# Turning attention probabilities by a trip over DRAM and VectorE instead of TensorE, with scores two tiles ahead

## The chip, the cores and the metric

One core of a Trainium2 chip runs the whole kernel. The metric is the device time of one launch in microseconds. Before the change the median of three runs was 490.21 us (490.07 to 491.41).

## The reference

The input x is 4 batches of 1024 tokens with 512 features, all fp32. Cut to what matters:

```python
mod = (silu(c) @ wmod).reshape(4, 6, 1, 512)        # sa, ca, ga, sb, cb, gb per batch
ga, gb = sign(ga) * max(|ga|, 0.25), sign(gb) * max(|gb|, 0.25)
h = layernorm(x) * (1 + ca) + sa
qf, kf = h @ Wq.T, h @ Wk.T                         # 64 columns each, the same for all 16 heads
attn = softmax(qf @ kf.T)                           # 1024 x 1024 per batch
x = x + ga * ((attn @ (h @ Wv.T)) @ Wo.T)
h = layernorm(x) * (1 + cb) + sb
x = x + gb * (h @ sum_r(factors[r]) / sqrt(8) + bias)
```

All heads share one probability matrix, so Wv and Wo are multiplied once into one 512x512 matrix, and the eight factors are summed once.

## The kernel before

The 4096 tokens are 32 tiles of 128, eight per batch, handled in 16 pairs. fp32 values go through TensorE as two roundings: a high part (`_hi`) and the rest (`_lo`, `rest()` at line 838), and `three()` multiplies hi x lo, lo x hi and hi x hi (lines 373 to 375).

A prologue makes the modulation vectors, the weights and the values and keys of the first batch. Then come 32 steps, one per tile t. Every engine runs its own hand-written order of the same step, and semaphores join them; most steps run in loops (`Fori`). In step t TensorE does, in order:

- `transpose_probs(t)`: eight 128x128 transpositions of the probabilities into two PSUM banks ps_t (line 379);
- in odd steps the query/key projection of a pair of the next batch, and in steps 0 to 23 the value projection of tile t+8;
- the scores of tile t+1 into ps_s (two banks, lines 447 and 448);
- the feed-forward of tile t-3 into ps_y;
- `attend(t)`: 24 matmuls into ps_o, which start when VectorE has made the first half of pt_lo.

ScalarE rounds ps_t to pt_hi (605), modulates x1 of tile t-2 (634), rounds the values, normalizes x1 of tile t-1 (693), modulates x of tile t+9 (634), takes the exponentials of tile t+1 (674, into the only buffer `probs`), and normalizes x of tile t+10 (642). VectorE gates the attention of tile t-1 (918), adds x (926), takes statistics (931, 935), turns x1 and x (961, 957), subtracts for pt_lo and the values' rest (838), takes the row maximum of tile t+1 (890), finishes the feed-forward (951), and splits h and h2 into a cast for the high part (855, 901) and a subtraction for the rest (838). GpSimd makes inverse deviations (1173 to 1177), and multiplies and adds the feed-forward's result (1189, 1192).

x and x1 are already turned by a trip. SP sends the normalized tile in 32-column blocks to DRAM (`blocks_out`, line 301) and fetches it with the blocks in another order (`blocks_in`, line 306); VectorE transposes all 32x32 blocks in one instruction; and ScalarE's modulation reads them in order and writes every fourth element. SP issues these in one queue with the loads of x (245) and stores of the result (252). In a step its order is: fetch x, send x1, store, fetch x1, send x, load.

The gates ga and gb of all four batches are broadcast over the partitions by SP (`spread_gate`, lines 266 and 268) into `gates`, 1 MB each.

Of the kernel before, what the change touches and what calls it, by code (L numbers as in the profile page):

```python
# [20 lines left out]
GATE_MADE = [12, 18]  # L21


def adaln_block(nc, x, wqk_t, wv, wo_t, factors, bias, c_t, wmod, out):
# [29 lines left out]
    assert (P, D, R, C, TB, B) == (128, 512, 64, 4, 8, 4) and KEYS == 2 * D  # L54
# [5 lines left out]
    x1_blocks = nc.dram_tensor("x1_blocks", [2, Q, P, P], F32, kind="Internal").ap()  # L60

    with ExitStack() as ctx:
# [24 lines left out]
        negmax = sb("negmax", [P, 2])  # L87
        rowsum = sb("rowsum", [P, 2])
        rden = sb("rden", [P, 2])
        bias_bc = sb("bias_bc", [P, D])  # L90
# [11 lines left out]
        gates = sb("gates", [P, 2, B, D])  # L102
        mod_rows = gates[0:B].rearrange("b a c d -> b (a c) d")
# [12 lines left out]
        with ExitStack() as setup:  # L116
            sb("under_parts", [P, TB, D], F32, setup)
            w_parts = [sb("w_part_0", [P, C, D], F32R, setup), sb("w_part_1", [P, C, D], F32R, setup)]
            sb("under_more", [P, TB, D], F32, setup)
            w_parts += [sb("w_part_2", [P, C, D], F32R, setup), sb("w_part_3", [P, C, D], F32R, setup)]  # L120
            sb("under_last", [P, TB, D], F32, setup)
            w_parts += [sb("w_part_4", [P, C, D], F32R, setup)]
            f_sum = sb("f_sum", [P, C, D], F32, setup)
        wmod_sb = [wmod_0, wmod_1, wmod_2]
# [17 lines left out]
        f_lo = sb("f_lo", [P, C, D], F32R)  # L142
        probs = sb("probs", [P, KEYS])
        qs_hi = sb("qs_hi", [P, 2 * P], F32R)
        qs_lo = sb("qs_lo", [P, 2 * P], F32R)
        h2_f = sb("h2_f", [P, C, P])
# [58 lines left out]
        qs_hi_done, qs_lo_done = sem("qs_hi_done"), sem("qs_lo_done")  # L205
        s_acc, max_done, exp_done = sem("s_acc"), sem("max_done"), sem("exp_done")
# [28 lines left out]

        block = ctx.enter_context(nc.Block())
# [3 lines left out]
        def _(sp):  # L240
# [21 lines left out]
            def spread_gate(i, vector):  # L262
# [3 lines left out]
                sp.dma_start(gate_rows[i], mod_rows[:, row_of[vector], :]).then_inc(gate_stored[i], 16)  # L266
                sp.wait_ge(gate_stored[i], 16)
                sp.dma_start(gates[:, i].rearrange("p b d -> p (b d)"), gate_rows[i].rearrange(
                    "b d -> (b d)").partition_broadcast(P)).then_inc(gate_loaded[i], 16)
# [25 lines left out]
            spread_gate(0, GA)  # L295
# [29 lines left out]
            def step(g, u, next_x=True, next_norm=True, store=True, load=False):  # L325
                t = 2 * g + u
                if next_x:
                    fetch_x(t + TB + 1, 1 - u)
                send_x1(t - 1, 1 - u)
                if u and store:  # L330
                    store_pair(g - 2)
                fetch_x1(t - 1, 1 - u)
                if next_norm:
                    send_x(t + TB + 2, u)
                if u and load:
                    wait_alone(sp, sp_passed, y_stored, 16 * (g - 1))
                    load_x(g - 2 + 2 * PB)

            step(0, 1, next_x=False, next_norm=False, store=False)
            step(1, 0, next_x=False, store=False)  # L340
            spread_gate(1, GB)
            step(1, 1, store=False)
            for u in range(2):
                step(2, u, load=True)
            with sp.Fori(3, PAIRS - 2 * PB + 2) as g:
                for u in range(2):
                    step(g, u, load=True)
            with sp.Fori(PAIRS - 2 * PB + 2, PAIRS - PB - 1) as g:
                for u in range(2):
                    step(g, u)  # L350
            step(PAIRS - PB - 1, 0, next_norm=False)
            step(PAIRS - PB - 1, 1, next_x=False, next_norm=False)
            with sp.Fori(PAIRS - PB, PAIRS - 1) as g:
                for u in range(2):
                    step(g, u, next_x=False, next_norm=False)
            step(PAIRS - 1, 0, next_x=False, next_norm=False)
            last = PAIRS - 1
            store_pair(last - 2)
# [10 lines left out]
        def _(pe):  # L369
# [36 lines left out]
            def modulation_columns(n, vectors):  # L406
                for i, v in enumerate(vectors):
                    for k in range(C):
                        at = (i * C + k) * B
                        last = nc.tensor.transpose(mod_t_banks[n][:, at:at + B], mod_rows[:, row_of[v], P * k:P * (k + 1)],  # L410
# [87 lines left out]
            def step(g, u, prep=True, following=True, older=True, late_x=None, ready=None):  # L498


                t = 2 * g + u
                transpose_probs(t)
                if prep and u:
                    pe.wait_ge(h_lo_done, t + TB + 1)
                    project_qk(g + PB)
                if late_x is not None:
                    late_x()
                if prep:
                    project_values(t + TB, u)
                if following:  # L510
                    scores(t + 1, 1 - u, g + u)
                if older:
                    feed_forward(t - 3)
                if ready is not None:
                    ready()
                attend(t, g)

# [56 lines left out]
            step(0, 0, older=False, late_x=transpose_first_late)  # L574
            step(0, 1, older=False, late_x=transpose_second_late, ready=lambda: pe.wait_ge(h_f_done, TB + 3))
            step(1, 0, older=False, late_x=transpose_third_late)
            pe.wait_ge(h_f_done, TB + 4)
            step(1, 1)
            with pe.Fori(2, PAIRS - PB) as g:
                for u in range(2):  # L580
                    step(g, u)
            with pe.Fori(PAIRS - PB, PAIRS - 1) as g:
                for u in range(2):
                    step(g, u, prep=False)
            step(PAIRS - 1, 0, prep=False)

            step(PAIRS - 1, 1, prep=False, following=False)
# [15 lines left out]
        def _(act):  # L603
# [68 lines left out]
            def exponentials(t, u):  # L672
                act.wait_ge(max_done, t + 1)
                nc.scalar.activation(probs[:], ps_s[:], ACT.Exp, bias=negmax[:, u:u + 1],  # L674
                                     accum_out=rowsum[:, u:u + 1]).then_inc(exp_done, 1)

            def probs_part(t, half):
                act.wait_ge(pt_ps, 2 * t + half + 1)
                rounded(pt_hi[:, HALF * half:HALF * (half + 1), :], ps_t[half][:]).then_inc(pt_hi_done, 1)
# [25 lines left out]
            def modulate_x1(t, b):  # L705
                if not isinstance(t, int) or t > 0:
                    wait_alone(act, act_passed, h2_lo_done, t)
                wait_alone(act, act_passed, x1b_turned, t + 1)
                modulate_turned(h2_f, x1b, b, 2).then_inc(h2_f_done, 1)

            def factor_parts():
                for half in range(2):
# [4 lines left out]
            def step(g, u, prep=True, next_x=True, next_norm=True, last_pair=False, after_x=True):  # L717
                t = 2 * g + u
                first = isinstance(g, int) and g == 0
                by_pe = isinstance(t, int) and t + TB + 1 in late_x_banks  # L720
                probs_part(t, 0)
                if prep and u:
                    qk(g + PB)
                probs_part(t, 1)
                if by_pe:
                    modulate_x(t + TB + 1, batch_of(g + u + PB), late_x_banks[t + TB + 1])
                if not first:
                    modulate_x1(t - 2, batch_of(g - 1))
# [589 lines left out]
```

## Time and profile before

| | |
|---|---|
| median of 3 runs | 490.21 us |
| profiled execution | 491.66 us, span 489.5 us |
| mean granted TensorE clock | 0.994 |
| TensorE, VectorE, ScalarE, GpSimd busy | 473.9, 370.0, 282.5, 196.3 us |
| DMA | 62.63 MB, mean 128 GB/s |

Busy time is the union of an engine's instructions; the span runs from the first to the last instruction. The profiled execution is one run, 1.45 us above the median; 2.2 us of it lie around the span. Instructions of one engine overlap by about 0.1 us when they follow each other directly, so a duration is a little more than the distance from start to start.

### The profile page before, as it was taken

The page shows a single profiled execution, that of the slowest core. Times are in us where ns is not written, and L with a number is a line of the kernel's source. Part 1 is how long each engine was busy: PE and PEld are TensorE (multiplying, and loading weights), DVE is VectorE, ACT ScalarE, POOL GpSimd, SP SyncE. Part 2 cuts the span into 40 slices and gives each one's busy share as a digit, 9 for nine tenths or more (in the row PEclk, how much of TensorE's full clock was granted, in tenths as well). Part 3 has the DMA queues.
Part 4 walks back from the last instruction along what each step waited for, and adds up shares of the span by engine and source line. Part 5 has one row for each costly group of instructions (what it writes and reads, how often), then busy time and mean ns, then how long its engine had stood idle before and what let it go on. Part 6 is the DMA issues. An engine that isn't in the chain of part 4 may idle for free.

```text
span 489.5 us, 9481 instructions
## 1 busy us (share of the span) xinstructions
PE 473.9 (97%) x2306; PEld 385.7 (79%) x2306; DVE 370.0 (76%) x688; ACT 282.5 (58%) x579; POOL 196.3 (40%) x286
## 2 busy tenths in 40 slices
PE   8999889999999999999999999999999999999985
PEld 3777658887888888888888888888888888888864
DVE  2896875888886877786878868687877587978775
ACT  2877655577574747466665747474765453554431
POOL 0475763414433424243434334242432533344344
PEclk9999998999999999999999999999999999999999
DMA  8968889754244252525243342535341212132212
GB/s 301 364 255 210 153 157 227 152 140 153 66 129 124 80 160 86 171 72 165 84 130 99 112 130 81 156 86 171 85 129 44 86 44 86 43 97 95 61 49 86
DMA packets 50818, 62.63 MB, mean 128 GB/s; under 512 B 2920, under 2 KB 29288, under 8 KB 50544
## 3 DMA queue, kind: packets, MB, share of 16 engines
q1 hardware_dynamic: 46848, 54.82, 35.1%
q0 software_dynamic: 3808, 7.34, 8.9%
q10 hardware_dynamic: 144, 0.26, 0.1%
q8 instruction: 7, 0.11, 0.1%
q14 instruction: 11, 0.09, 0.1%
HBM read 40.90 MB, written 21.51 MB: 128 GB/s over the span
## 4 chain that ended last, share of the span: by engine, by line
PE 77%; DVE 7%; issue 6%; ACT 3%; DMA 3%; POOL 2%; SPq 0%; ACTq 0%; DVEq 0%; POOLq 0%
PE ps_o L373 11%; PE ps_o L375 11%; PE ps_o L374 11%; PE ps_t L379 6%; PE ps_y L373 5%; PE ps_y L375 5%; PE ps_y L374 5%; PE ps_v L373 5%; PE ps_v L374 4%; PE ps_v L375 4%; PE ps_s L447 3%; PE ps_s L448 3%; PE ps_qk L373 1%; PE ps_qk L375 1%; PE ps_qk L374 1%
## 5 line engine op out<-in xcount | busy, mean ns | idle before, releaser
L373 PE MATMUL ps_o<-v_lo,pt_hi 128*128 (+1 forms) x256 | 100.6, 393 | 1.8 <-DVE pt_lo L838 1.8
L1173 POOL TENSOR_SCALAR ve<-mv 128x1 f32<-128x1 f32 x64 | 14.9, 233 | 216.1 <-DVE mv L935 188.3
L375 PE MATMUL ps_o<-v_hi,pt_hi 128*128 (+1 forms) x256 | 99.8, 390 | 0.0
L374 PE MATMUL ps_o<-v_hi,pt_lo 128*128 (+1 forms) x256 | 99.7, 389 | 0.0
L605 ACT ACTIVATE pt_hi<-ps_t 128x512 fp32r<-128x512 f32 x64 | 36.1, 597 | 75.1 <-PE ps_t L379 74.8
L634 ACT ACTIVATE h_f<-x1b,mod_t 128x128 f32<-128x128 f32 x120 | 53.2, 595 | 44.8 <-DVE x1b L961 44.8
L918 DVE SCALAR_TENSOR_TENSOR attn<-ps_o,rden,gates 128x512 f32<-128x512 f32 x32 | 24.0, 751 | 58.8 <-PE ps_o L375 57.4
L373 PEld LDWEIGHTS ps_o<-v_lo,pt_hi 128*128 128x128 f32 x256 | 48.1, 188 | 14.2 <-issue 3.6
L375 PEld LDWEIGHTS ps_o<-v_hi,pt_hi 128*128 128x128 f32 x256 | 48.0, 188 | 10.1
L374 PEld LDWEIGHTS ps_o<-v_hi,pt_lo 128*128 128x128 f32 x256 | 48.1, 188 | 9.7
L838 DVE TENSOR_TENSOR h_lo<-h_f,h_hi 128x512 fp32r<-128x512 f32 (+1 forms) x67 | 51.5, 782 | 1.2
L373 PE MATMUL ps_y<-f_lo,h_hi 128*128 128x512 f32 (+1 forms) x124 | 48.4, 390 | 0.3 <-DVE h_lo L838 0.3
L375 PE MATMUL ps_y<-f_hi,h_hi 128*128 128x512 f32 (+1 forms) x124 | 47.9, 386 | 0.0
L374 PE MATMUL ps_y<-f_hi,h_lo 128*128 128x512 f32 (+1 forms) x124 | 47.9, 386 | 0.0
L1189 POOL TENSOR_TENSOR ffn<-ffn,gates 128x512 f32<-128x512 f32 x30 | 40.5, 1350 | 16.9 <-DVE ffn L951 15.3
L373 PE MATMUL ps_v<-wvo_lo,h_hi 128*128 128x512 f32 x112 | 45.5, 406 | 0.0
L374 PE MATMUL ps_v<-wvo_hi,h_lo 128*128 128x512 f32 x112 | 44.3, 396 | 0.0
L375 PE MATMUL ps_v<-wvo_hi,h_hi 128*128 128x512 f32 x112 | 44.1, 394 | 0.0
L1192 POOL TENSOR_TENSOR x_ring<-ffn,x_ring 128x512 f32 (+1 forms) x30 | 39.8, 1325 | 10.2 <-POOL ffn L1189 10.2
L674 ACT ACTIVATE probs<-ps_s,negmax 128x1024 f32<-128x1024 f32 x32 | 35.6, 1114 | 12.8 <-DVE negmax L890 12.7
L1175 POOL TENSOR_TENSOR rstd<-ve,minus_half 128x1 f32<-128x1 f32 x64 | 39.9, 623 | 5.3
L838 DVE TENSOR_TENSOR pt_lo<-ps_t,pt_hi 128x512 fp32r<-128x512 f32 x64 | 41.7, 665 | 0.1
(170 smaller groups left out, 1004.4 us busy)
## 6 DMA issues: line engine op xcount, KB each, us to landing
x_blocks<-xn SPq DMA_DIRECT2D x50, 256.0 KB, 2.3
x_ring<-in_x SPq DMA_DIRECT2D x16, 512.0 KB, 3.8
x1b<-x_blocks SPq DMA_DIRECT2D x30, 256.0 KB, 2.7
result<-x_ring SPq DMA_DIRECT2D x15, 512.0 KB, 3.0
f_sum<-in_factors POOLq DMA_DIRECT2D x14, 512.0 KB, 7.3
wmod<-in_wmod SPq DMA_DIRECT2D x12, 512.0 KB, 6.9
xb<-x_blocks SPq DMA_DIRECT2D x20, 256.0 KB, 2.7
gates<-gate_rows SPq DMA_DIRECT2D x2, 1024.0 KB, 6.2
```

What stands on the lines that cost most here:

```text
L373: nc.tensor.matmul(acc, a_hi, b_lo, start=first, stop=False)
L374: nc.tensor.matmul(acc, a_lo, b_hi, start=False, stop=False)
L375: return nc.tensor.matmul(acc, a_hi, b_hi, start=False, stop=last)
L379: last = nc.tensor.transpose(acc[:, P * i:P * (i + 1)], source[:, P * (base + i):P * (base + i + 1)], ident[:])
L605: return nc.scalar.activation(to, source, ACT.Identity)
L634: last = nc.scalar.activation(to[:, k, :].rearrange("p (c b) -> p b c", b=Q), turned[:, k], ACT.Identity, scale=mod_t[:, b, v + 1, k:k + 1 ...
L674: nc.scalar.activation(probs[:], ps_s[:], ACT.Exp, bias=negmax[:, u:u + 1], accum_out=rowsum[:, u:u + 1]).then_inc(exp_done, 1)
L838: return nc.vector.tensor_tensor(to, whole, full(hi), ALU.subtract)
L918: nc.vector.scalar_tensor_tensor(out=attn[:], in0=ps_o[:], scalar=rden[:, u:u + 1], in1=gates[:, 0, b, :], op0=ALU.mult, op1=ALU.mult).the ...
L1175: nc.gpsimd.tensor_tensor(rstd[:, one], ve[:, one], minus_half[:], ALU.pow).then_inc(rstd_done, 1)
L1189: nc.gpsimd.tensor_tensor(ffn[:, 0:D], ffn[:, 0:D], gates[:, 1, b, :], ALU.mult).then_inc(gated_done, 1)
L1192: nc.gpsimd.tensor_tensor(tile, ffn[:, 0:D], tile, ALU.add).then_inc(y_done, 1)
```

## The change

For 24 of the 32 tiles (all but 0 to 4, 8, 16 and 24) the probabilities are no longer turned by TensorE. ScalarE writes the exponentials in 32-column blocks, SP sends them to `p_blocks` in DRAM and fetches them in the other order into `pb` (two slots), VectorE transposes 128x1024 in one instruction at the end of the step before, ScalarE rounds from pb to pt_hi and VectorE subtracts for pt_lo, both with every fourth element.

- Scores: those of tile t+2 are made in step t, after the feed-forward. The first two tiles of a batch are exceptions: the first is scored in the last step of the batch before, ahead of its attention, the second in the same step behind its attention. Its maximum and exponentials open the next step on VectorE and ScalarE.
- The casts of h and h2 to their high parts move from VectorE to ScalarE.
- SP's order in a step: fetch x, fetch probabilities, send x1, store, send probabilities, send x, fetch x1, load.
- The gates are held for two batches at a time: 256 KB are broadcast per gate and batch, the first ones where 1 MB was, the later ones in steps 5, 13 and 21.
- GpSimd multiplies the result ahead of the statistics of x1 and adds it behind them.
- The query parts of a pair are made in odd steps instead of even ones. All steps are unrolled.

```diff
+def turned_by_pe(t):
+    return t <= LAST_EARLY or t % PER_BATCH == 0          # LAST_EARLY = 4, PER_BATCH = 8
+def scored_in(t):
+    if t < LAST_EARLY:
+        u = t + 1
+    elif t % PER_BATCH == PER_BATCH - 2:
+        return None
+    else:
+        u = t + (1 if t % PER_BATCH == PER_BATCH - 1 else 2)
+    return u if u < TILES else None
+def scored_last_in(t):
+    opens = t == LAST_EARLY - 1 or t % PER_BATCH == PER_BATCH - 1
+    return t + 2 if t >= 0 and opens and t + 2 < TILES else None
...
+        def turned_probs(t):
+            return pb[:, trips_of(t) & 1, :].rearrange("p (b k c) -> p k b c", b=Q, c=BLK)
...
+            def spread_gate(i, b):
+                sp.wait_ge(gate_stored[i], 16)
+                if b:
+                    sp.wait_ge(gate_loaded[i], 16 * b)
+                if b > 1:
+                    sp.wait_ge((attn_done, gated_done)[i], TB * (b - 1))
+                sp.dma_start(gates[:, i, b & 1, :], gate_rows[i, b].partition_broadcast(P)).then_inc(gate_loaded[i], 16)
...
+            def send_p(t):
+                n = trips_of(t)
+                sp.wait_ge(exp_done, t + 1)
+                if n > 1:
+                    sp.wait_ge(pb_loaded, 16 * (n - 1))
+                sp.dma_start(p_blocks[n & 1].rearrange("a p x -> p a x"),
+                             probs[:].rearrange("p (a x) -> p a x", a=Q)).then_inc(p_out, 16)
+            def fetch_p(t):
+                n = trips_of(t)
+                sp.wait_ge(p_out, 16 * (n + 1))
+                sp.wait_ge(pt_lo_done, 2 * (t - 1))
+                sp.dma_start(pb[:, n & 1, :],
+                             p_blocks[n & 1].rearrange("a (c b) x -> (a c) (b x)", b=Q)).then_inc(pb_loaded, 16)
...
             # TensorE, a step
+                if turned_by_pe(t):
+                    transpose_probs(t)
...
+                if t >= 3:
                     feed_forward(t - 3)
+                if scored_in(t) is not None:
+                    scores_of(scored_in(t))
                 attend(t, g)
+                if scored_last_in(t) is not None:
+                    scores_of(scored_last_in(t))
...
             # ScalarE
+                to, source = in_quarters(pt_hi)[:, here], turned_probs(t)[:, here]     # a trip tile
...
+            def h_upper(q, u):
+                act.wait_ge(h_f_done, q + 1)
+                rounded(h_hi[:, :, here], h_f[:]).then_inc(h_hi_done, 1)
...
             # VectorE
+                    last = rest(in_quarters(pt_lo)[:, here], turned_probs(t)[:, here], in_quarters(pt_hi)[:, here])
...
+            def turn_p(t):
+                n = trips_of(t)
+                dve.wait_ge(pb_loaded, 16 * (n + 1))
+                nc.vector.transpose(pb[:, n & 1, :], pb[:, n & 1, :]).then_inc(pb_turned, 1)
```

VectorE's new order in a step: maximum of a tile scored last, gate, query/key rest, add, statistics, turn x1, first pt_lo, values, statistics of x, turn x, second pt_lo, maximum, rests of h and h2, feed-forward's end, query parts, turn of pb.

## Rows read from the trace of the kernel before

**Rows 1.** The page, part 1: busy time, share, instructions of each engine.
```profile
PE 473.9 (97%) x2306; PEld 385.7 (79%) x2306; DVE 370.0 (76%) x688; ACT 282.5 (58%) x579; POOL 196.3 (40%) x286
```
**Rows 2.** Stretches: PE, PEld, DVE, ACT, POOL busy, clock, DMA share, GB/s.
```profile
136.32:190.12 53.80, 53.80 (x267) 45.15 (x265) 41.28 (x80) 33.09 (x68) 20.57 (x32) 1.00 0.39 117
392.10:463.20 71.10, 71.10 (x340) 58.20 (x339) 57.74 (x91) 34.58 (x69) 27.05 (x35) 1.00 0.24 71
```
**Rows 3.** Chain that ended last, in order of time: start, us, what.
```profile
190.12 0.87 PE ps_t L379 x8
204.25 0.87 PE ps_t L379 x8
216.93 0.87 PE ps_t L379 x8
```
**Rows 4.** Timeline of TensorE around the transpositions, mid-kernel and tail: start, duration.
```profile
203.85 0.39 PE L375 MATMUL ps_o<-v_hi,pt_hi 128*128 x1
...
204.88 0.48 PE L373 MATMUL ps_v<-wvo_lo,h_hi 128*128 128x512 f32 x1
...
412.23 1.03 PE L379 MATMUL ps_t<-ident,probs 128*128 128x128 f32 x8
...
416.75 0.48 PE L373 MATMUL ps_o<-v_lo,pt_hi 128*128 x1
```
**Rows 5.** Groups of VectorE in 136.32 to 190.12: busy, mean ns, idle before.
```profile
L918 DVE SCALAR_TENSOR_TENSOR attn<-ps_o,rden,gates 128x512 f32<-128x512 f32 x4 | 3.0, 752 | 8.7 <-PE ps_o L375 8.7
...
L926 DVE TENSOR_TENSOR x_ring<-attn,x_ring 128x512 f32 x4 | 2.8, 693 | 1.0 <-DVE attn L918 1.0
```
**Rows 6.** Groups of the whole span, by form.
```profile
L890 DVE TENSOR_REDUCE negmax<-ps_s 128x1 f32<-128x1024 f32 x32 | 38.8, 1214 | 0.0
...
L961 DVE STREAM_TRANSPOSE x1b<-x1b 128x512 f32<-128x512 f32 x30 | 20.9, 696 | 0.3 <-DMA x1b<-x_blocks 0.3
...
L855 DVE CAST h_hi<-h_f 128x512 fp32r<-128x512 f32 x32 | 15.2, 474 | 3.5 <-ACT h_f L610 3.4
...
L605 ACT ACTIVATE w_part<-wmod 128x512 fp32r<-128x512 f32 x12 | 6.6, 629 | 0.0
...
L838 DVE TENSOR_TENSOR v_lo<-wv_raw,v_hi 128x512 fp32r<-128x512 f32 x4 | 2.7, 680 | 6.7 <-ACT v_hi L605 6.7
```
**Rows 7.** Instructions on the tile ps_t: ns min/median/max, first and last start.
```profile
L838 DVE TENSOR_TENSOR pt_lo<-ps_t,pt_hi x64: 650/668/693, 74.9 to 467.2; 128x512 fp32r<-128x512 f32 x64
```
**Rows 8.** Timeline of ScalarE: four modulations, plain and strided.
```profile
99.19 1.51 ACT L610 ACTIVATE h_f<-ps_y,mod_t 128x128 f32<-128x128 f32 x4
...
154.46 1.77 ACT L634 ACTIVATE h_f<-x1b,mod_t 128x128 f32<-128x128 f32 x4 [2.45 <-DVE x1b L961]
```
**Rows 9.** DMA issues of the page: count, KB each, median us to landing.
```profile
x_blocks<-xn SPq DMA_DIRECT2D x50, 256.0 KB, 2.3
x_ring<-in_x SPq DMA_DIRECT2D x16, 512.0 KB, 3.8
x1b<-x_blocks SPq DMA_DIRECT2D x30, 256.0 KB, 2.7
```
**Rows 10.** Timeline of the tail, VectorE and GpSimd.
```profile
398.80 1.29 POOL L1189 TENSOR_TENSOR ffn<-ffn,gates 128x512 f32<-128x512 f32 x1 [1.55 <-DVE ffn L951]
...
398.98 1.66 DVE L838 TENSOR_TENSOR h_lo<-h_f,h_hi 128x512 fp32r<-128x512 f32 x1
...
412.75 0.75 DVE L918 SCALAR_TENSOR_TENSOR attn<-ps_o,rden,gates 128x512 f32<-128x512 f32 x1 [2.71 <-PE ps_o L375]
...
415.93 1.25 DVE L838 TENSOR_TENSOR pt_lo<-ps_t,pt_hi 128x512 fp32r<-128x512 f32 x2
```
**Rows 11.** Timeline around step 3: SP, VectorE and TensorE.
```profile
111.14 0.34 SPq L268 DMA_DIRECT2D gates<-gate_rows  x1
...
116.52 0.71 DVE L957 STREAM_TRANSPOSE xb<-xb 128x512 f32<-128x512 f32 x1 [1.87 <-DMA xb<-x_blocks]
...
117.95 0.47 PE L373 MATMUL ps_o<-v_lo,pt_hi 128*128 128x512 f32 x1 [1.03 <-DVE pt_lo L838]
```

More of the change, by code:

```diff
@@ L21, with pe_turns_of, trips_of, queries_in @@
 GATE_MADE = [12, 18]
+LAST_EARLY = 4
+TILES, PER_BATCH = 32, 8
+def turned_by_pe(t):
+    return t <= LAST_EARLY or t % PER_BATCH == 0
+def pe_turns_of(t):
+    return sum(turned_by_pe(u) for u in range(t))
+def trips_of(t):
+    return t - pe_turns_of(t)
+def scored_in(t):
[9 more added lines that the diff above has]
+    return t + 2 if t >= 0 and opens and t + 2 < TILES else None
+def queries_in(t):
+    pair = (t + 3) // 2 if t % 2 and t >= LAST_EARLY - 1 else t // 2 + 1 if t % 2 == 0 and t < LAST_EARLY - 1 else None
+    return pair if pair is not None and 2 * pair < TILES else None
 def adaln_block(nc, x, wqk_t, wv, wo_t, factors, bias, c_t, wmod, out):
@@ L337, in step @@
+                if u and 2 <= g < PAIRS - 2 * PB + 2:
+                    sp.wait_ge(y_stored, 16 * (g - 1))
                     load_x(g - 2 + 2 * PB)
[L339 to L356, printed above, removed]
+            for t in range(T):
+                step(t)
+                if t == 1:
+                    store_gate(1, GB)
+                if t == 2:
+                    spread_gate(1, 0)
+                if t < T - TB and t % TB == TB - 3:
+                    for i in range(2):
+                        spread_gate(i, t // TB + 1)
@@ L573, in _ @@
             pe.wait_ge(h_f_done, TB + 1)
-            step(0, 0, older=False, late_x=transpose_first_late)
-            step(0, 1, older=False, late_x=transpose_second_late, ready=lambda: pe.wait_ge(h_f_done, TB + 3))
-            step(1, 0, older=False, late_x=transpose_third_late)
+            step(0, transpose_first_late)
+            step(1, transpose_second_late, lambda: pe.wait_ge(h_f_done, TB + 3))
+            step(2, transpose_third_late)
             pe.wait_ge(h_f_done, TB + 4)
[L578 to L587, printed above, removed]
+            for t in range(3, T):
+                step(t)
             pe.wait_ge(x2n_done, T - 1)
@@ L771, in prep_pair @@
                     if u and first_scores:
-                        exponentials(0, 0)
+                        exponentials(0)
                     values(q, prologue_v[u])
@@ L968, in step @@
+            def step(t):
+                g, u = t // 2, t % 2
+                q = t + TB + 1
+                if scored_last_in(t - 1) is not None:
+                    row_max(scored_last_in(t - 1))
+                if t:
+                    gate_attention(t - 1, 1 - u, batch_of((t - 1) // 2))
+                if t < T - TB and u:
+                    qk_rest(g + PB)
+                if t:
                     add_x(t - 1)
                     x1_sums(t - 1, 1 - u)
-                if not first:
+                if t < T - TB and u:
+                    k_rest(g + PB)
+                if t >= 2:
```

356 lines of the change are left out of this document (183 added, 173 removed).

## The prediction

> **What bounds the kernel now.** I read the page first, then stretches, the chain of waits, and the timelines of one step. The page gives TensorE 473.9 us of 489.5, VectorE 370.0, ScalarE 282.5 [rows 1]. An average hides the stages, so next the stretches: over four tiles in mid-kernel (53.80 us) TensorE is busy for all 53.80, VectorE for 41.28, ScalarE for 33.09, DMA for 0.39 of its time; with no projections left (71.10 us) TensorE is still busy throughout [rows 2]. The chain is TensorE's own work, step after step: 14.13 us for a step with a query/key projection, 12.68 for one without [rows 3]; in the tail 71.10/7, about 10.15. What leaves TensorE there is time saved, as long as another engine doesn't take its place.
>
> **Transpositions removed.** Eight of them stand between the attention of one tile and the next work. The last attention matmul starts at 203.85; with the usual 0.23 from start to start the next would follow at 204.08, but the projection starts at 204.88 [rows 4]. That is 0.80; the chain gives the eight 0.87, with what the first matmul behind them loses [rows 3]. I take 0.87. Eight times the duration of one (over 0.27) would say 2.2 and is wrong: matmuls overlap. 24 tiles make 20.9 us as the ceiling. They fall in two stages: tiles 5 to 7, 9 to 15 and 17 to 23 (17) beside projections, tiles 25 to 31 (7) in the tail.
>
> **VectorE, in the first 17.** In the four-tile stretch it waits 8.7 us for the attention's last matmul [rows 5]; so it needs (53.80 - 8.7)/4 = 11.27 us per tile, and has 2.18 free. TensorE's period falls from 13.45 to 12.58, which leaves 1.31. The edits:
> - Two casts per tile go to ScalarE. One takes 474 ns alone [rows 6], less in line; -0.75 for two.
> - A 32x32 transposition of 1024 columns comes. 512 columns take 696 ns; a reduction of 1024 takes 1214 [rows 6]. Bounds 1.13 to 1.39 (twice 696); I take 1.2, the reduction's.
> - The two roundoff subtractions read SBUF instead of PSUM and read and write every fourth element. No strided VectorE row exists. Nearest: an SBUF source without stride, 680 ns beside 668 from PSUM [rows 6, 7]. ScalarE's four strided modulations take 1.77, four plain ones 1.51 [rows 8]: 0.26 over 512 columns, part of it the end of the last. Bounds 0 and a doubled element time, 0.52 (what 512 more columns cost, 1214 - 696 [rows 6]); I take 0.2, two of them 0.4.
> - A new exposure: with two SBUF inputs VectorE can stand behind GpSimd. At 398.98 such a subtraction took 1.66 instead of 0.68; GpSimd's multiplication ran from 398.80 to 400.09, and the rest came after that [rows 10]. None of the 64 subtractions from PSUM went over 693 ns [rows 7]. GpSimd has two 1.3 us operations and small ones per tile. Bounds 0 and 2 x 0.97 = 1.94 per tile; I take one half-hit, 0.5, as GpSimd's addition (after the statistics of x1) falls near the second subtraction.
>
> The Trainium skill, "SBUF — State Buffer", section "SBUF: two separate sides", states it as a rule: a VectorE operation with two SBUF inputs and a GpSimd operation that reads SBUF exclude each other for a whole instruction. The trace agrees (1.66 against 0.68), and by the rule this change is exposed twice per tile: that is the rival that ends slower. The same page's section on the DMA port swizzle puts fp32 strides up to four elements down as free; by it the 0.4 above would be 0. ScalarE's rows (0.26 over 512 columns) speak against quite free.
>
> Sum 11.27 - 0.75 + 1.2 + 0.4 + 0.5 = 12.62 beside TensorE's 12.58. The two meet. Two engines so close that hand each other work lose a little to waiting; I put 0.2 on it, an estimate from the 0.25 that VectorE waits for its own result before an addition, 1.0 over four [rows 5]. So 12.8 instead of 13.45: 0.65 x 17 = 11.1 us.
>
> **ScalarE** in the same stage: 8.27 busy per tile, plus two casts (629 ns from SBUF, 0.53 in line, and 0.2 for its own result: 1.5 together), plus 0.2 to 0.4 on two roundings: about 10.2 to 10.5 of 12.58 [rows 2, 6]. Hidden; if that cover goes, only its place in the cycle below counts.
>
> **The trip.** Scores stand two tiles ahead, so the exponentials of tile t+2 end near the end of step t. 512 KB take 3.8 us [rows 9], out and in 7.6 and some 0.7 of issue and waits, against a step of 12.6; the transposition is the last thing VectorE does in step t+1. Hidden by about 3 us. The new waits and what stands behind them: VectorE's turn of pb waits for the fetch, and behind it the gate and with it the next attention's buffer; SP's sending waits for the exponentials, and behind it stand the sending of x and the fetch of x1; the exponentials wait for the sending before, long landed. If the cover of 3 us goes, each us more is one on VectorE. A megabyte more per tile beside 1.6 now (117 GB/s [rows 2]) lifts the DMA share from 0.39 to some 0.65: no bound.
>
> **SP's order.** Fetching x1 now stands behind the sending of the probabilities and of x. That closes a cycle: fetch 2.7, VectorE's turn 0.7, ScalarE sees it 0.47, modulates x1 1.57, normalizes x1 0.7, modulates x 1.57, casts 0.7 and 0.5, exponentials 1.1, normalizes x 0.75, issues 0.95 in the code's order [rows 6, 8, 9]: 11.7, plus what the 512 KB ahead in the queues adds: 0 to 1.5 (3.8 - 2.3). With 0.5, 12.2, it stays under 12.6. ScalarE waited 2.45 for VectorE's turn before its modulation [rows 8]: the path has slack of that size and no more.
>
> **Batch ends (steps 6 to 8, 14 to 16, 22 to 24).** Scores of a batch's second tile run after the attention of the last tile before. Step 6 loses them (0.91), step 8 gains them: zero. In step 8 VectorE and ScalarE each begin with one more operation (1.2, 1.1), but 6 us of projection and feed-forward lie ahead of the attention; zero.
>
> **The tail.** There VectorE's chain from the attention's end to the first pt_lo decides. The step's transpositions start at 412.23; VectorE's attn starts at 412.75, its first pt_lo at 415.93 and ends near 416.58, 4.35 us after the slot; TensorE starts the attention at 416.75, 4.52 after it [rows 4, 10]. Without transpositions it would be ready at 3.65 and waits for the 4.35. Of 0.87 only some 0.15 is left, with the stride 0.1: six steps, 0.6. Step 31 has no scores, so even now less than 4.35 lies ahead of its attention: nothing. Step 24 gets the second scores (0.91) and VectorE's maximum ahead of gate, add and statistics: attention at about 1.4 + 1.2 + 3.8 = 6.4 instead of 4.52, a loss of 1.9, of which step 22 gave 0.9. Tail and its opening: 0.6 + 0.9 - 1.9 = -0.4.
>
> **The start.** At 111.14 SP issued the 1 MB broadcast of the gates, behind a store that it had waited for, and only then fetched x: the turn of x waited 1.87 us and TensorE 1.03 [rows 11]. The store now stands a step earlier, and 256 KB are broadcast: 1.0 gained. Later broadcasts of 256 KB stand in steps 5, 13, 21: hidden. The unrolled loops I price at 0: no row shows a wait for code, and none excludes one.
>
> **Sum.** 11.1 - 0.4 + 1.0 = 11.7 us. The profiled execution took 491.66 (span 489.5 and 2.2 around it), 1.45 above the median of 490.21; against the median, 478.5.
>
> **Rivals.**
> - Everything hidden: period 12.58, no hits by GpSimd. 14.8 - 0.4 + 1.0 = 15.4: 474.8. For it: VectorE's numbers meet it within 0.1. Against: my sum has VectorE level with TensorE.
> - SP's cycle decides: the full 1.5 us of queueing makes 13.2 per tile. 0.25 x 17 - 0.4 + 1.0 = 4.9: 485. For it: x1's fetch is now the last of SP's step. Against: 256 KB landed in 2.3 to 2.7 in the median, with 512 KB transfers in the same queues [rows 9].
> - Slower: GpSimd's lock hits both subtractions of each tile, 0.97 each. VectorE needs 11.27 + 0.45 + 0.4 + 1.94 = 14.06, against 13.45 before: 0.61 x 17 = 10.4 lost; start and tail give 0.6 back: 500. It decides as soon as a subtraction costs 0.87 more than before ((2.18 - 0.45)/2). For it: 1.66 in rows 10. Against: every one has to be hit, and GpSimd is idle for 33 of 53.80 us (20.57 busy) [rows 2].
> - The change doesn't do what it says (TensorE spared, but each removed slot filled by an equal wait): 490.
>
> **Chances.** Forecast 0.42, everything hidden 0.18, SP's cycle 0.18, no net change 0.07, slower 0.15. The measurement tells 0.3% (1.5 us) from nothing. Faster: 0.42 + 0.18 + 0.17 = 0.77; same 0.08; slower 0.15. The forecast's own range is 474 to 482. Leaving 0.15 above and 0.05 below: 472 to 489.
>
> **What would show it.** Right: a mid-kernel step pair of some 25.6 us instead of 26.81; VectorE busy over 11 us per tile, hardly waiting for the attention's last matmul; tail steps of about 10; the stall at 117.95 gone. Subtractions on pb near 0.85 us with a few at 1.2 to 1.7. Wrong: pt_lo over 1.5 on average (the lock), turns of x1 waiting for DMA in each step (SP's cycle), turns of pb waiting for DMA (the trip isn't hidden), or TensorE idle at the batch ends.

## The result, and the profile after

The changed kernel is slower: 503.5 us (median of 4 runs, 499.85 to 503.82) against 490.14 (median of 4 runs, 489.68 to 491.41) on the same chip, a ratio of 1.025 (95% interval 1.020 to 1.030). Forecast were 478.5 us and a range of 472 to 489. The profiled execution has a span of 502.0 us; before it was 489.5, so 12.5 us are to be explained.

Part 1 of the page after, for [rows 1], and the head of its chain of waits:

```profile
PE 461.0 (92%) x2114; PEld 366.3 (73%) x2114; DVE 400.0 (80%) x659; ACT 339.9 (68%) x632; POOL 216.1 (43%) x286
...
DVE 30%; PE 23%; DMA 17%; issue 13%; ACT 9%; POOL 6%; SPq 1%; ACTq 0%; DVEq 0%; POOLq 0%
```

TensorE is busy 12.9 us less than before, and the span is 12.5 us longer: 25 us of idle time on TensorE are new. No single engine took its place. The chain before was TensorE at 77%; now it goes round over VectorE, DMA, ScalarE and GpSimd.

Which stage? I count a step from one start of `attn` on VectorE to the next. Stretches of the kernel after, cut at the `attn` of tiles 4, 23 and 31; the columns are those of [rows 2]:

```profile
0.00:137.17 137.17, 128.19 (x626) 97.36 (x627) 101.62 (x186) 92.04 (x187) 63.21 (x92) 1.00 0.74 192
137.17:396.70 259.53, 247.77 (x1130) 201.94 (x1129) 220.08 (x355) 194.99 (x355) 106.94 (x147) 0.99 0.57 183
396.70:484.84 88.14, 74.90 (x310) 59.21 (x309) 66.68 (x97) 49.05 (x82) 38.00 (x40) 0.96 0.47 149
484.84:502.00 17.16, 10.13 (x55) 7.81 (x53) 11.65 (x22) 3.83 (x9) 7.94 (x9) 0.92 0.17 63
```

The same cuts before lie at 136.63, 392.45 and 473.16. Inside the 19 steps from tile 4 to tile 23 the steps fall in two kinds, so I part them too: the eight around a batch's end (6, 7, 8, 14, 15, 16, 22, 23) and the 11 others. All numbers are differences of those `attn` starts in the profiled execution:

```
                      start    11 steps (each)    8 steps   tail (8)   end
before               136.63    149.42 (13.58)     106.40     80.71    16.34
after                137.17    148.53 (13.50)     111.00     88.14    17.16
change                +0.5      -0.9               +4.6      +7.4     +0.8
forecast              -1.0      -7.15              -3.9      +0.4      -
```

(The forecast's 0.65 for each of 17 steps: 11 of the first kind, 6 of the second, where steps 8 and 16 keep their transpositions. A negative number is time saved.) So the ordinary step hardly got shorter, by 0.08 us instead of 0.65; counted between the first attention matmuls on TensorE it is 0.27 (13.33 instead of 13.60). The pairs of steps 9+10, 11+12, 17+18 and 19+20 took 26.28, 27.05, 27.28 and 26.84 us, against 26.81 before and a forecast of some 25.6. The batch ends, priced at zero beside the 0.65, and the tail lost 12.0 us.

**The ordinary step** is a closed cycle. One turn of it in the chain of waits of the kernel after (start, us, what), from one fetch of x1 to the next:

```profile
207.24 2.94 DMA x1b<-x_blocks
210.21 0.04 DVE x1b L1067
210.24 0.60 issue
210.84 0.14 DVE mv L1040
210.98 0.57 DVE pt_lo L932
211.56 0.30 issue
211.86 0.68 DVE v_lo L932
212.54 0.60 DVE stats L935
...
213.68 1.70 DVE pt_lo L932
215.38 1.13 DVE negmax L991
...
216.80 1.07 POOL ve L1275
...
217.94 0.58 POOL rstd L1277
...
218.73 0.27 POOL nmr L1279
219.01 0.83 ACT xn L715
...
219.92 0.36 SPq L362
...
220.47 3.04 DMA x1b<-x_blocks
```

From 207.24 to 220.47 are 13.23 us; the turns beside it in the chain took 13.19, 13.05 and 13.81, and the table's eleven steps 13.50 on average. SP issues the fetch of x1 behind the sending of x, which waits for ScalarE's `xn`, for GpSimd's three small operations, for VectorE's `mv` of x (L939); and that stands behind both subtractions (`pt_lo`) and the row maximum, which stand behind the turn of the x1 fetched before. The x1 to be fetched had been in DRAM since about 216.5: SP issued its own sending at 214.09 (x_blocks<-xn lands in 2.4).

**The subtractions.** Instructions on the tile pt_lo after, to be read beside [rows 7]:

```profile
L932 DVE TENSOR_TENSOR pt_lo<-pb,pt_hi x48: 1035/1064/1710, 141.6 to 478.8; 128x512 fp32r<-128x512 f32 x48
L932 DVE TENSOR_TENSOR pt_lo<-ps_t,pt_hi x16: 652/656/691, 74.5 to 400.2; 128x512 fp32r<-128x512 f32 x16
```

The stride costs 0.41 each (1064 against 656; with plain columns, experiment 1, those from pb take 656 too). It lies on pt_lo and pt_hi; pb itself is read in runs of 32. 13 of the 48 stand at 1.5 to 1.71, one in each of 13 mid-kernel steps, always the second, behind GpSimd's addition. From the timeline of the kernel after:

```profile
200.21 1.29 POOL L1297 TENSOR_TENSOR x_ring<-ffn,x_ring 128x512 f32<-128x512 f32 x1
...
200.75 1.69 DVE L932 TENSOR_TENSOR pt_lo<-pb,pt_hi 128x512 fp32r<-128x512 f32 x1
```

**The batch end.** SP's queue in step 6 of the kernel after, and what its chain of waits shows there:

```profile
150.35 0.36 SPq L362 DMA_DIRECT2D x_blocks<-xn  x1
150.89 0.42 SPq L367 DMA_DIRECT2D x1b<-x_blocks  x1
151.44 0.37 SPq L299 DMA_DIRECT2D x_ring<-in_x  x1
151.91 0.91 SPq L329 DMA_DIRECT2D gates<-gate_rows  x2
153.01 0.32 SPq L367 DMA_DIRECT2D xb<-x_blocks  x1
```

```profile
153.01 6.25 DMA xb<-x_blocks
...
159.29 0.04 DVE xb L1063
159.32 0.60 issue
159.93 1.05 DVE pt_lo L932
...
161.02 0.52 PE ps_o L448
```

The two gate broadcasts are issued right ahead of the fetch of x. That fetch of 256 KB, 3.0 us in the median, takes 6.25, and behind the turn of x in VectorE's program stands the second subtraction, for which TensorE idles 2.40 us. The idleness costs once more, as the stretches around it show (the seventh number is the granted clock):

```profile
158.60:161.00 2.40, 0.02 (x1) 0.00 (x0) 1.71 (x3) 0.96 (x3) 0.00 (x0) 1.00 0.81 291
161.00:164.90 3.90, 3.88 (x10) 3.10 (x11) 2.45 (x5) 2.67 (x6) 1.38 (x4) 0.56 0.06 16
164.90:168.00 3.10, 3.10 (x21) 2.79 (x20) 1.47 (x4) 0.89 (x3) 0.97 (x1) 1.00 0.54 154
```

After 2.4 us without work TensorE ran 3.4 of the next 3.9 us at the lower of its two levels (1.2 GHz; matmuls 0.43 apart instead of 0.23): some 1.7 us more.

**The tail.** GpSimd's groups from 396.70 to 484.84 (mean ns, idle before):

```profile
L1277 POOL TENSOR_TENSOR rstd<-ve,minus_half 128x1 f32<-128x1 f32 x8 | 8.7, 1090 | 0.7
L1275 POOL TENSOR_SCALAR ve<-mv 128x1 f32<-128x1 f32 x8 | 6.9, 865 | 39.0 <-DVE mv L1040 39.0
```

The same two took 567 and 222 ns in the kernel before. They work on one column; it is the lock in reverse. In each step both subtractions stand right behind `mv`, and the two short operations come in their time. That is 1.17 us more per step between the statistics of x1 and what follows from x1. In four of the eight steps the chain that ended last runs over them (from 409.42, 421.38, 431.49 and 454.64); in the others it runs over the subtractions and the attention.

### The profile page after: what moved, and what is told of

It reads as the page before. It is cut to its first block, busy times and chain, and to the rows that moved or that the text cites. A ratio compares the mean times of both kernels' runs of the same rounds, so it can differ in the third digit from the quotient of the medians.

```text
span 502.0 us, 7290 instructions
## 1 busy us (share of the span) xinstructions
PE 461.0 (92%) x2114; PEld 366.3 (73%) x2114; DVE 400.0 (80%) x659; ACT 339.9 (68%) x632; POOL 216.1 (43%) x286
## 4 chain that ended last, share of the span: by engine, by line
DVE 30%; PE 23%; DMA 17%; issue 13%; ACT 9%; POOL 6%; SPq 1%; ACTq 0%; DVEq 0%; POOLq 0%
DMA x1b<-x_blocks 8%; DVE pt_lo L932 7%; DMA xb<-x_blocks 6%; PE ps_o L448 4%; PE ps_o L450 4%; PE ps_o L449 4%; DVE negmax L991 3%; DMA x_blocks<-xn 3%; DVE h_lo L932 2%; POOL rstd L1277 2%; ACT xn L715 2%; POOL ve L1275 2%; DVE stats L935 2%; DVE x_ring L1031 2%; ACT probs L755 2%
## 5 line engine op out<-in xcount | busy, mean ns | idle before, releaser
L1275 POOL TENSOR_SCALAR ve<-mv 128x1 f32<-128x1 f32 x64 | 37.1, 579 | 213.3 <-DVE mv L1040 140.5
L448 PE MATMUL ps_o<-v_lo,pt_hi 128*128 128x512 f32 x256 | 104.0, 406 | 25.5 <-DVE pt_lo L932 25.4
L450 PE MATMUL ps_o<-v_hi,pt_hi 128*128 128x512 f32 x256 | 101.9, 398 | 0.0
L449 PE MATMUL ps_o<-v_hi,pt_lo 128*128 128x512 f32 x256 | 101.7, 397 | 0.0
L678 ACT ACTIVATE pt_hi<-pb 128x512 fp32r<-128x512 f32 x48 | 49.1, 1128 | 18.1 <-PE ps_o L450 13.1
L932 DVE TENSOR_TENSOR h_lo<-h_f,h_hi 128x512 fp32r<-128x512 f32 (+1 forms) x67 | 44.3, 688 | 20.3 <-ACT h_hi L678 19.8
L932 DVE TENSOR_TENSOR pt_lo<-pb,pt_hi 128x512 fp32r<-128x512 f32 x48 | 58.3, 1228 | 0.0
L450 PEld LDWEIGHTS ps_o<-v_hi,pt_hi 128*128 128x128 f32 x256 | 49.2, 192 | 10.7
L1277 POOL TENSOR_TENSOR rstd<-ve,minus_half 128x1 f32<-128x1 f32 x64 | 44.9, 702 | 5.3
L707 ACT ACTIVATE h_f<-xb,mod_t 128x128 f32<-128x128 f32 x80 | 35.2, 589 | 7.2 <-DVE xb L1063 7.2
L991 DVE TENSOR_REDUCE negmax<-ps_s 128x1 f32<-128x1024 f32 x32 | 38.9, 1217 | 0.1
```

What stands on the lines that cost most here:

```text
L448: nc.tensor.matmul(acc, a_hi, b_lo, start=first, stop=False)
L449: nc.tensor.matmul(acc, a_lo, b_hi, start=False, stop=False)
L450: return nc.tensor.matmul(acc, a_hi, b_hi, start=False, stop=last)
L678: return nc.scalar.activation(to, source, ACT.Identity)
L707: last = nc.scalar.activation(to[:, k, :].rearrange("p (c b) -> p b c", b=Q), turned[:, k], ACT.Identity, scale=mod_t[:, b, v + 1, k:k + 1 ...
L932: return nc.vector.tensor_tensor(to, whole, full(hi), ALU.subtract)
```

## The experiments

Each kernel is the one after with the edit shown; times are medians of 4 runs, or of 10 where they spread, the ratio is against the kernel before measured beside it (489.6 to 490.3 us), with its 95% interval. Lengths of steps and stretches come from the traced run of each kernel, which lies up to 3.6 us from its median. An ordinary step is the mean of the table's eleven. "Full" means that all of the reference is computed.

**1. The two suspects on VectorE.** Theory: the stride and the lock make VectorE too slow. Rival: the order of SP's queue does. Here the roundings and subtractions write and read columns in the order in which they lie (the queries within a tile then stand in another order than the reference's); then GpSimd's multiplication and addition do one column instead of 512; then both.

```diff
-            return tile[:].rearrange("p k (c b) -> p k b c", b=Q)
+            return tile[:].rearrange("p k (b c) -> p k b c", b=Q)
```
```diff
-  nc.gpsimd.tensor_tensor(ffn[:, 0:D], ffn[:, 0:D], gates[:, 1, b & 1, :], ALU.mult)
+  nc.gpsimd.tensor_tensor(ffn[:, 0:1], ffn[:, 0:1], gates[:, 1, b & 1, 0:1], ALU.mult)
```

> The changed kernel with one line other: pt_hi and pt_lo of the 24 trip tiles are written and read in 32-column runs instead of every fourth element (the queries of a tile stand in another order, so the attention rows are not the reference's). Theory A (the stride doubles the element time on VectorE and ScalarE, and with GpSimd's lock that makes these two the bound): pt_hi falls from 1.13 to about 0.62 us, an unblocked pt_lo from 1.04 to 0.69, and the time falls by 8 to 15 us, to 488 to 495. Theory B (SP's order, the late fetch of x1, is the bound): the durations fall the same way, but the time by less than 3 us. Theory C (GpSimd's lock alone decides): VectorE's second pt_lo still ends with GpSimd's addition, less than 5 us.

> The changed kernel, with GpSimd's multiplication and addition of the result cut to one column (the rest of that computation is left out). Strides stay. Theory A: pt_lo's mean falls from 1.23 to about 1.05, 0.37 per tile of VectorE in 24 tiles and more in the tail, where these operations hit qs_lo and h_lo too: 6 to 12 us less, 491 to 497. Theory B: less than 3 us. Theory C: 12 to 20 us less, below the kernel before.

> Both edits: plain columns, and GpSimd's two operations cut to one column (both computations are changed as there). Theory A: VectorE and ScalarE fall under TensorE's period, 12.6 us per mid-kernel tile: 474 to 482, more than the sum of the two alone or equal to it. Theory B: over 495, since SP's order is untouched. Theory C: the same as GpSimd's part alone, within 3 us.

Plain columns: 487.69 (0.9955, 0.993 to 0.998). Short GpSimd: 493.48 (1.0065, 1.004 to 1.009). Both: 481.98 (0.983, 0.979 to 0.987). The stride is worth 15.8 us, most of the 19.7 that VectorE spends on it (48 x 0.41): VectorE lies in the way. But with the full-size GpSimd operations gone the ordinary step still took 13.29 instead of 13.50. Its chain of waits says why:

```profile
204.86 3.39 DMA x1b<-x_blocks
208.28 0.03 DVE x1b L1067
...
211.99 1.76 ACT h_f L707 x4
213.78 0.64 ACT h_hi L678
...
215.05 0.69 DVE h_lo L932
215.74 0.31 DVE ffn L1057
216.06 0.83 ACT xn L715
...
217.98 3.03 DMA x1b<-x_blocks
```

The same cycle, 13.12 us, now on its leg over ScalarE's modulations: the lock on `pt_lo` lies beside another leg of nearly the same length. What this cure gained lies mostly in the tail (85.05 instead of 88.14) and in the end (14.25 instead of 17.16), in part because the operations themselves are gone.

**2. Which engine's stride?** Plain columns on ScalarE's roundings alone, and on VectorE's subtractions alone (there with the changed order of queries; in the first, high part and rest still add up to the right probability in its place).

> The changed kernel with plain columns on ScalarE alone: pt_hi is written in 32-column runs, VectorE still reads and writes every fourth element (hi and rest no longer belong together, so the attention isn't the reference's). Takes 1.0 us per tile from ScalarE. If ScalarE's path holds the time: 8 to 14 us less, 490 to 496. If VectorE does: under 4 us less.

> The changed kernel with plain columns on VectorE alone (hi and rest don't belong together here either). An unblocked pt_lo falls from 1.04 to 0.65; the second of a tile still ends after GpSimd's addition, so about 0.4 to 0.8 per tile. If VectorE holds the time: 8 to 14 us less. If ScalarE's path does: under 4 us less. If the closed chain over both does: about half of the 16 us each, 494 to 498.

ScalarE alone: 501.79 (1.023, 1.017 to 1.028), 1.7 us under the kernel after, within its spread, though a strided rounding takes 1128 ns and a plain one 622. VectorE alone: 487.23 (0.9935, 0.991 to 0.996), the whole gain of the first experiment.

**3. SP's order.** The fetch of x1 goes right behind the store, ahead of the sending of the probabilities and of x. Full.

```diff
                     store_pair(g - 2)
+                if 1 <= t < T - 1:
+                    fetch_x1(t - 1, 1 - u)
                 if scored_in(t) is not None and not turned_by_pe(scored_in(t)):
                     send_p(scored_in(t))
                 if 12 <= t + TB + 2 < T:
                     send_x(t + TB + 2, u)
-                if 1 <= t < T - 1:
-                    fetch_x1(t - 1, 1 - u)
```

> The changed kernel with SP's old order: the fetch of x1 stands right behind the store, ahead of the sending of the probabilities and of x. Everything is computed. Theory A: x1b's 10.2 us of waits for DMA go, but VectorE and ScalarE stay the bound: 0 to 4 us less. Theory B: 8 to 15 us less. It can also lose: the fetch waits for the landing of x1's blocks, and the probabilities are then sent up to 2 us later; if that decides, turns of pb wait for DMA, and the time rises.

> The changed kernel with plain columns (the queries of a trip tile stand in another order) and SP's old place for the fetch of x1. The stride alone gave 16 us, the order alone 10. If both only feed one closed chain over VectorE, ScalarE and SP (theory A with B as one of its links), the second cure finds little left: 0 to 4 us less than plain columns alone, 483 to 488. If they are separate costs (theory D), their gains add: 475 to 480.

493.24 (1.006, 1.003 to 1.008): 10.3 us from the order of one DMA issue. The eleven ordinary steps fell to 12.90 each, with stride and lock still there, and their chain runs mostly on TensorE's matmuls again. So the cycle had bounded them. With plain columns as well: 483.71 (0.989, 0.984 to 0.994); the two don't add up (15.8 and 10.3 give 19.8).

**4. The gates' broadcasts.** `spread_gate` for the next batch in steps 3 and 6 of a batch, one each, behind the fetch of the probabilities, instead of both in step 5. Full.

```diff
+                if t < T - TB and t % TB in (3, 6):
+                    spread_gate(int(t % TB == 6), t // TB + 1)
...
-                if t < T - TB and t % TB == TB - 3:
-                    for i in range(2):
-                        spread_gate(i, t // TB + 1)
```

> The changed kernel with only the broadcasts of the next batch's gates put elsewhere (one in step 3, one in step 6 of a batch, behind the fetch of the probabilities). Everything is computed. The changed kernel's steps 6 and 7 took 3.9 us more than the kernel before's, 14 and 15 1.6 more, 22 and 23 1.4 more. If the broadcasts do that: 3 to 7 us less, 497 to 500. If it is the order of scores at the batch end: under 2.

496.15 (1.011, 1.008 to 1.014), 7.4 us. The eight batch-end steps went from 111.00 to 104.67 us (106.40 before); the other 11 kept 13.48. In step 6 the fetch of x landed in 3.87 us instead of 6.25, and the granted clock stayed at its upper level. Two issues in each of three steps were more than the whole loss of 4.6 us at the batch ends.

**5. Casts back on VectorE.**

```diff
-                    h_upper(q, 1 - u)
-                if t >= 2:
-                    h2_upper(t - 2)
```

(on ScalarE; on VectorE each stands ahead of its subtraction, h2's behind `ffn_out`). Full.

> The changed kernel with the two casts of h and h2 back on VectorE (h2's behind the feed-forward's end). Everything is computed. It takes 1.1 us per tile from ScalarE and puts 0.75 on VectorE. If VectorE is the tighter of the two (my sum had it so): 3 to 10 us more. If the path over ScalarE (roundings of 1.13, modulations, casts) is the longer one: the time falls by up to 6.

510.88 (1.041, 1.038 to 1.044): 7.4 us worse. An ordinary step took 14.28 instead of 13.50, 0.78 for two casts where the prediction had 0.75; the eight batch-end steps fell by 2.1 in all.

**6. All four cures together**: plain columns, short GpSimd, x1 first, gates spread.

> The changed kernel with plain columns (queries in another order), GpSimd's two operations cut to one column (left out but for it), x1's fetch early and the gates spread: every cost found so far taken away, the trip, the casts and the two-ahead scores kept. If these are the causes, TensorE's period stands: 12.5 us per mid-kernel tile, and the time is what I forecast for all hidden, 472 to 478. If it stays over 480, something else holds TensorE, and it is in the order itself (odd steps of 14 to 15 us while SP's queue joins the waits).

471.45 (0.962, 0.959 to 0.964). Its stretches from `attn` of tile 4 to 23 to 31:

```profile
136.61:378.17 241.56, 241.56 (x1131) 202.33 (x1130) 199.99 (x354) 179.83 (x355) 56.27 (x146) 1.00 0.61 196
378.17:455.44 77.27, 71.72 (x310) 56.92 (x309) 58.93 (x97) 42.69 (x82) 15.00 (x41) 1.00 0.54 170
```

In the first of them TensorE is busy throughout again, and the 19 steps take 14.26 us less than before: 0.84 for each of the 17 tiles, where the prediction had 0.87 as TensorE's saving. The trip over DRAM, the 32x32 turn and the two casts on ScalarE are all in this kernel, and all hidden. (ScalarE's roundings are plain in it; experiment 2 has them plain alone, at 1.7 us.)

**7. Can it be had in full?** First the order made by the DMA: four fetches of 32 partitions in runs of 1 KB put the columns in place, so that nothing is strided; then with the cures of 3 and 4; then, on top of these, the tail's tiles turned by TensorE as before; or instead of that the sending of the probabilities issued by ScalarE behind its exponentials. All full.

```diff
-                sp.dma_start(pb[:, n & 1, :],
-                             p_blocks[n & 1].rearrange("a (c b) x -> (a c) (b x)", b=Q)).then_inc(pb_loaded, 16)
+                for a in range(Q):
+                    sp.dma_start(pb[BLK * a:BLK * (a + 1), n & 1, :].rearrange("c (b x) -> c b x", b=Q),
+                                 p_blocks[n & 1, a].rearrange("(b c) x -> c b x", b=Q)).then_inc(pb_loaded, 16)
```

> The changed kernel with the order of the queries mended where it costs no engine: SP fetches the probabilities in four transfers of 32 partitions, four runs of 1 KB for each partition instead of one of 4 KB, so that pt_hi and pt_lo are written in 32-column runs. Everything is computed. If the stride was the cost: as plain columns alone, 486 to 490. If four transfers of shorter runs land much later than the one did (3.5 us): turns of pb wait for DMA, 490 to 498.

> As the four fetches, with SP's old place for x1, and the two 256 KB broadcasts of the next batch's gates no longer both ahead of step 6's fetches: one behind the fetch of the probabilities in step 3 of a batch, one in step 6. Everything is computed. In the changed kernel xb took 6.25 us to land behind them, and with plain columns VectorE waited 2.5 and TensorE 2.0 there. Expected: that wait gone three times, 4 to 8 us less than the version with the four fetches. If steps 6 and 7 are long for another reason (the scores of two tiles in a row): less than 2.

> As the version before it, but tiles 25 to 31 turned by TensorE again, with scores one tile ahead from step 23 on. Everything is computed. My forecast priced the trip in the tail at about 0; the changed kernel lost 7.4 us there (step lengths 9.5 to 13.5 beside 9.6 to 10.4). If strides were all of it: within 2 us of the version before. If the tail loses to GpSimd's lock and the long way from statistics to normalization as well: 2 to 5 less. Against it: 0.87 of TensorE per tile comes back, at most 6 us more.

> The version with four fetches, x1's fetch early and the gates spread (485.5), with the sending of the probabilities issued by ScalarE right behind its exponentials instead of by SP. Everything is computed. In that version odd steps took 14.4 to 16.2 us because the transposition of pb or the fetch of x came late: SP's sendings stand behind a fetch that waits for a landing. If SP's one queue is what joins the waits: odd steps at 13.3 to 13.8, 478 to 482. If ScalarE's time (0.4 for each issue) or the DMA engines are the limit: within 2 us of 485.5.

Four fetches alone: 498.44 (1.0175, 1.012 to 1.023), just over the upper range expected and 10.7 us over the one fetch with plain columns; the traces have it in the batch ends (117.94 us for the eight steps against 107.13). SP has three more issues to make in each step. Which of the two, issues or short runs, does it wasn't tried. With x1 first and gates spread: 485.51 (0.992, 0.990 to 0.993), a little faster than both kernels. Tail by TensorE: 484.45 (0.988, 0.985 to 0.991). Sending from ScalarE: 484.84 (0.988, 0.985 to 0.991). These three can't be told apart: the last two spread over more than 3 us.

**8. The transposition writes in order.** One fetch; VectorE's 32x32 transposition itself writes every fourth column, so that the roundings and subtractions are plain; x1 first, gates spread. Full. Then the same with the two subtractions right behind each other.

```diff
-                nc.vector.transpose(pb[:, n & 1, :], pb[:, n & 1, :])
+                nc.vector.transpose(pb[:, 1, :].rearrange("p (k c b) -> p b k c", b=Q, c=BLK),
+                                    pb[:, 0, :].rearrange("p (b k c) -> p b k c", b=Q, c=BLK))
```
```diff
                 probs_rest(t, 0)
-                if t < LAST_EARLY:
-                    probs_rest(t, 1)
+                probs_rest(t, 1)
```

> The changed kernel with x1's fetch early and the gates spread, and VectorE's transposition writing every fourth column itself, from slot 0 of pb to slot 1; the two roundings and the two subtractions are then fully contiguous, and one transfer of 4 KB runs fetches. Everything is computed. One strided pass of 1024 elements instead of two on each engine. If a strided write costs VectorE 0.76 ns more per element (0.39 over 512), the transposition takes 1.24 + 0.8 = 2.0, and the time is 477 to 483. If the transposition already moves an element per cycle whatever the stride: 1.24, and 474 to 479.

> As the one before, with both halves of pt_lo right behind each other on VectorE, ahead of the values' rest and the statistics of x, so that GpSimd's addition no longer falls on the second half but on operations with a PSUM or a single input. Everything is computed. In the changed kernel the second half took 1.7 instead of 1.04 nearly each time. Expected: second halves at 0.65, 2 to 6 us less. Against it: GpSimd's statistics then wait behind them (ve took 1.87 in the tail behind two subtractions), and x1's normalization comes later: within 1 us or slower.

In order: 486.80 (0.994, 0.991 to 0.997), over the 477 to 483 expected. The instructions on pb show that the price of the stride only moved:

```profile
L1074 DVE STREAM_TRANSPOSE pb<-pb x24: 1985/2010/2064, 135.3 to 460.0; 128x1024 f32<-128x1024 f32 x24
```

2010 ns instead of 1235, where two subtractions saved 2 x 0.41. Together: 499.79 (1.019, 1.016 to 1.023), 13.0 us worse where 2 to 6 less were expected, though no subtraction met the lock any more (the longest 689 ns). The waits of the two kernels from tile 4 to 23, first in order, then together:

```profile
DVE h_lo L933 <- ACT h_hi L679: 11.0, 19, 2.6
```

```profile
DVE h_lo L933 <- ACT h_hi L679: 28.0, 19, 2.9
```

The second subtraction had stood in the time in which ScalarE modulates x for VectorE. Moved away, it leaves 0.9 us more of waiting per step. Avoiding the lock in that way costs more than the lock.

## Why the prediction was wrong, point by point

- **TensorE's saving**, 0.87 per tile: right. Busy time fell by 12.9 us although some stretches ran at the lower clock, and experiment 6 has 0.84 for each of the 17 tiles.
- **VectorE's sum.** Casts -0.75: 0.78 in experiment 5. Turn of pb 1.2: 1.24. Stride 0.2 each: measured 0.41, twice the term, within the bounds of 0 to 0.52. The Trainium skill, "SBUF — State Buffer", section "Door 1: The DMA port swizzle", would have had 0; the 1064 against 656 ns decide against it. Lock 0.5 per tile: 13 hits of some 0.62 over 17 tiles, 0.47. VectorE's busy time from tile 4 to 23 rose by 26.65 us, 1.57 for each of 17 tiles, where the terms made 1.35. This sum was off by 0.2, and alone would have cost 4 us, not 25.
- **SP's order: the first step that failed.** I put the cycle at 11.7 and followed it over ScalarE's program only: 7.3 from the start of the turn of x1 to the start of the normalization of x. Measured was 8.8 (210.21 to 219.01) on the leg over VectorE (two subtractions, v_lo, statistics, maximum) and GpSimd, to which the stride, the lock and its reverse all add. So 13.2 for a turn of the cycle: the value that the rival on SP's cycle had, for another reason (queueing). Experiment 3 opens the cycle, and the ordinary step falls from 13.50 to 12.90.
- **Batch ends: the second.** "Later broadcasts of 256 KB stand in steps 5, 13, 21: hidden" named no cover, and there was none: they stood right ahead of a fetch that VectorE's in-order program waits for. The eight steps took 4.6 us more instead of 3.9 less; experiment 4 returns 6.3 of these 8.5. The profile before had shown this at 116.52 and 117.95 [rows 11]; I booked its removal as a gain, and not its return.
- **The tail: the third.** The sum, a loss of 0.4, had 0.1 for the stride and nothing for the lock. Measured is a loss of 7.4: beside the 2 x 0.41 and GpSimd's 1.17 per step, TensorE waited 13.2 us for pt_lo. Its granted clock fell to the lower level twice, for 3.4 us each (mean 0.96 over 88.14 us: at most 3.5 us of the loss), after waits of 2.33 and 3.51 us; after one of 2.60 us it didn't. Plain columns bring the tail to 80.04 (80.71 before), x1 first alone to 84.30, short GpSimd alone to 85.05. So plain columns alone end the whole loss there, and each of the other two a part of it.
- **Start**, a gain of 1.0: measured is a loss of 0.5. The stall of [rows 11] is gone, as predicted, and TensorE's attention of tile 3 starts at 116.26 instead of 117.95. But behind it stand the scores of tile 5, which I had priced for step 24 only: the next attention starts 14.15 us later instead of 12.77. What is left of the gain there is 0.3 (130.41 against 130.72), and the `attn` of tile 4, where the table cuts, stands behind the new turn of pb on VectorE:

```profile
135.75 1.23 DVE L1072 STREAM_TRANSPOSE pb<-pb 128x1024 f32<-128x1024 f32 x1
...
137.17 0.75 DVE L1023 SCALAR_TENSOR_TENSOR attn<-ps_o,rden,gates 128x512 f32<-128x512 f32 x1 [0.15 <-DVE rden L1019]
```

- **The rivals.** All hidden (474.8): what experiment 6 shows, 471.45, once four costs are gone. Slower by the lock (500): near in time, not in its mechanism. It asked for a hit on each subtraction; 13 of 48 were hit, and with GpSimd's two long operations cut short the ordinary step gained 0.2. The rule behind it (the Trainium skill, "SBUF — State Buffer", "SBUF: two separate sides": whichever of the two starts first holds the ports for its whole instruction) agrees with the trace in both directions. The direction that I left out, a short GpSimd operation held up by VectorE, lies in the chain of the tail in half of its steps. No net change (490): not the time, but it is what the ordinary steps did, with pairs of 26.86 us on average against 26.81.

The size of the parts as single cures, from 503.5: stride 15.8, x1's order 10.3, GpSimd 10.0, gates 7.4; all four 32.0. They don't add up, and cures of one cycle share their gain.

Open: why x1 first with plain columns has ordinary steps of 13.28 where each alone has 12.9; and how the tail's loss divides between the stride itself and the lock and the clock that come with it. For either, no run parts them.

## What to carry to other kernels

When an engine at 100% is relieved, don't compare sums of engines only: close each cycle that runs through the program orders of several engines and a DMA queue, over every leg, and compare its length with the new period. For each DMA that is issued in a new place, look at what stands right behind it in that queue and who waits for it. A fetch whose data are long there should never stand behind a sending that waits for the end of the step.

## What the runs showed of the hardware

- A last-dimension stride of four fp32 elements isn't free: VectorE's subtraction of 512 columns (one input and the output strided) 656 to 1064 ns, ScalarE's rounding 622 to 1128, VectorE's transposition of 1024 columns with a strided output 1235 to 2010.
- GpSimd operations on one column, 222 and 567 ns, took up to 1.87 and 1.28 us beside VectorE's subtractions with two SBUF inputs.
- A fetch of 256 KB behind two broadcasts of 256 KB to all partitions: 6.25 us against 3.0 in the median, and 3.87 with the broadcasts moved behind it.
- Four fetches of 128 KB in 1 KB runs land one by one as fast as one of 512 KB in 4 KB runs (median 3.2 against 3.5 us), and still the kernel is 10.7 us slower with them.
